# Four-layer graph network on one Trainium2 core: seven quarter products for the first linear product of layer 1

## What is computed

```python
h = jnp.maximum(_layernorm(x, axis=-1), 0.0)
def _gcn_layer(x, adj, W, b):
    support = jnp.einsum('bnf,fh->bnh', x, W)
    return jnp.einsum('bnm,bmh->bnh', adj, support) + b
h = jax.nn.relu(_gcn_layer(h, adj, W1, b1))
h = jax.nn.relu(_gcn_layer(h, adj, W2, b2))
x = x + _gcn_layer(h, adj, W3, b3)
```

## Time and profile before

| | |
|---|---|
| median of 3 runs | 2630.46 us (2630.12 to 2632.95) |
| profiled execution | 2627.68 us, its span 2625.9 us |
| granted TensorE clock | 0.999 |
| busy, share of the span | PE 99%, PEld 83%, DVE 70%, ACT 54%, POOL 56% |
| layer 0 | to about 909 us |
| layer 1 | about 909 to 1609 us |
| layer 2 | about 1609 to 2235 us |
| layer 3 | to the end |

### The profile page before, as it was taken

One profiled execution on the slowest core, in us unless ns is written; L12 is line 12 of the kernel. 1 busy time (PEld: TensorE's weight loads), 2 busy tenths in 40 slices (PEclk: granted clock), 3 DMA queues, 4 the chain that ended last, 5 costly groups with the idle time before them and its releaser, 6 DMA issues.

```text
span 2625.9 us, 44958 instructions
## 1 busy us (share of the span) xinstructions
PE 2591.7 (99%) x12938; PEld 2173.1 (83%) x12938; DVE 1843.3 (70%) x4093; ACT 1406.1 (54%) x2623; POOL 1472.8 (56%) x2283
## 2 busy tenths in 40 slices
PE   7999999999999999999999999999999999999999
PEld 6888888888888888888888888888888887788887
DVE  8877777777777766666666666666667676677776
ACT  5443444434444555454545455666566665666665
POOL 6544454444444654333333335777777767877776
PEclk9999999999999999999999999999999999999999
DMA  3111111111111321111111112222222223444443
GB/s 117 55 47 40 38 42 38 42 44 38 35 41 38 98 85 51 52 50 52 50 52 50 52 50 87 84 93 76 98 76 96 78 80 118 134 140 152 151 136 120
DMA packets 145389, 195.25 MB, mean 74 GB/s; under 512 B 55475, under 2 KB 55475, under 8 KB 145334
## 3 DMA queue, kind: packets, MB, share of 16 engines
q1 hardware_dynamic: 138560, 183.55, 21.4%
q10 hardware_dynamic: 6774, 11.03, 1.3%
HBM read 127.42 MB, written 67.11 MB: 74 GB/s over the span
## 4 chain that ended last, share of the span: by engine, by line
PE 93%; DVE 2%; POOL 2%; issue 1%; ACT 1%; DMA 0%; ACTq 0%; POOLq 0%; DVEq 0%
PE ps L584 27%; PE ps L586 27%; PE ps L585 26%; PE ps L601 6%; PE ps L626 4%; PE ps L604 2%; POOL w_lo L1476 1%; DVE row_lo L1122 0%; ACT row_hi L842 0%; POOL row_lo L1476 0%; PE ps L765 0%; PE ps L772 0%; DMA raw<-w_t 0%; POOL x_res L1589 0%; DVE stats L1216 0%
## 5 line engine op out<-in xcount | busy, mean ns | idle before, releaser
L584 PE MATMUL ps<-w_hi,col_hi 128*128 128x512 f32 x2432 | 970.0, 399 | 4.9 <-DVE w_lo L1122 3.8
L586 PE MATMUL ps<-w_hi,col_lo 128*128 128x512 f32 x2432 | 950.3, 391 | 0.0
L585 PE MATMUL ps<-w_lo,col_hi 128*128 128x512 f32 x2432 | 948.4, 390 | 0.0
L584 PEld LDWEIGHTS ps<-w_hi,col_hi 128*128 128x128 f32 x2432 | 457.6, 188 | 98.4 <-issue 7.9
L586 PEld LDWEIGHTS ps<-w_hi,col_lo 128*128 128x128 f32 x2432 | 457.0, 188 | 98.9
L585 PEld LDWEIGHTS ps<-w_lo,col_hi 128*128 128x128 f32 x2432 | 458.4, 188 | 87.5
L842 ACT ACTIVATE col_hi<-ps 128x512 fp32r<-128x512 f32 (+1 forms) x512 | 291.1, 578 | 225.3 <-PE ps L604 116.0
L1500 POOL TENSOR_TENSOR var_eps<-moments,eps_ln 128x1 f32<-128x1 f32 x256 | 51.2, 200 | 481.0 <-DVE moments L1139 480.8
L1476 POOL TENSOR_TENSOR row_lo<-normed,row_hi 128x512 fp32r<-128x512 f32 x160 | 207.4, 1297 | 197.2 <-ACT row_hi L842 195.3
L601 PE MATMUL ps<-adj_both,row_hi 128*128 128x256 f32 x1024 | 246.6, 329 | 0.2 <-DVE deg L1177 0.2
L1126 DVE TENSOR_TENSOR wide<-ps,col_hi 128x512 f32<-128x512 f32 x256 | 175.5, 686 | 78.7 <-ACT col_hi L842 76.1
(11 more groups left out here) (181 smaller groups left out, 4798.6 us busy)
## 6 DMA issues: line engine op xcount, KB each, us to landing
out<-x_res SPq DMA_DIRECT2D x256, 256.0 KB, 2.0
x_in<-out SPq DMA_DIRECT2D x192, 256.0 KB, 2.8
x_res<-out SPq DMA_DIRECT2D x128, 256.0 KB, 3.2
x_in<-x SPq DMA_DIRECT2D x64, 256.0 KB, 2.6
adj_in<-adj_t SPq DMA_DIRECT2D x96, 64.0 KB, 2.3
raw<-wk ACTq DMA_DIRECT2D x14, 256.0 KB, 3.6
raw<-w ACTq DMA_DIRECT2D x12, 256.0 KB, 2.7
raw<-w_t ACTq DMA_DIRECT2D x10, 256.0 KB, 4.2
```

Of the source, the lines that this page charges most:

```text
L584: nc.tensor.matmul(out_ap, lhs_hi, rhs_hi, start=start, stop=False, **checks)
L585: nc.tensor.matmul(out_ap, lhs_hi, rhs_lo, start=False, stop=False, **checks)
L586: return nc.tensor.matmul(out_ap, lhs_lo, rhs_hi, start=False, stop=stop, **checks)
```

## The change

**Seven quarter products.** For each pair of slots u = (a, b) of layer 1, the 24 matmuls of lin0 with 512 columns become seven products of a 256 x 256 quarter of W1 (two rows of 128, `narrow`) with 128 rows of one side: six matmuls of 256 columns each. The blocks are the left and right half of the features of slot a and slot b; the products are named and combined as in layers 2 and 3.
- adj0: ACT copies the first half to wide and not to col_hi, DVE's adj0hi adds the second half there in one step; the new adj0c copies it to col_hi (ACT) and subtracts for col_lo (POOL), for odd slots only 256 columns.
- sums0 (DVE, four steps of 256 columns per pair), sumsplit0 (ACT and POOL, two halves of 512 columns each).
- bias0 per pair: two copies of 256 columns; the second half holds the difference of the two bias halves, made once on POOL.
- q1, p6, s5 (ACT copies of 256 columns out of PSUM), c11, c22, c12 (DVE, 256 columns each), rows0 (the rectifier on ACT, in two halves for odd slots), rows0hi (DVE, likewise).

**Orders.** order_gcn, last_gcn and last_hyper are new lists; those of the other layers stay.

**Weights.** In layer 0's last group four raw blocks are loaded at once; seven quarters (B11, B21, B22 and four differences T, made on DVE) are split there and then the eight blocks of W2 and W3: 15 splits in place of 12. The bias is prepared there. STAGING is told by step and not by place for layer 1, steps 9, 10 and 11 move from group 1 to group 15, and EARLY_AT puts the blocks that take the place of the quarters last; they wait for p4 of the last pair.

The diff, cut to its core (the lists of last_hyper, last_gcn and the counting of semaphores are left out):

```diff
+        ("resid", 0), ("p1", 0), ("q1", 0), ("p2", 0), ("adj0", 3), ("p6", 0), ("s5", 0), ("p5", 0), ("p7", 0),
+        ("bias0", 1), ("rows0", 0), ("c11", 0), ("p3", 0), ("adj0hi", 3), ("sums0", 1), ("p1", 1), ("c12", 0),
+        ("p2", 1), ("sumsplit0", 1), ("c22", 0), ("q1", 1), ("p4", 0), ("rows0hi", 0), ("rows0hi", 1),
+        ("rows0", 1), ("adj1hi", 0), ("resid", 1), ("stats_n", 0), ("c11", 1), ("adj0c", 3), ("c22", 1),
+        ("c12", 1), ("adj1hi", 1), ("adj1", 0), ("p6", 1), ("s5", 1), ("bias1", 0), ("p5", 1), ("resid", 2),
+        ("adj1", 1), ("p7", 1), ("rows0hi", 2), ("norm_n", 0), ("rows0", 2), ("stats_n", 1), ("p3", 1),
+        ("resid", 3), ("bias1", 1), ("lin1hi", 0), ("rows0", 3), ("lin1", 0), ("adj1hi", 2), ("p4", 1),
+        ("adj1", 2), ("bias1", 2), ("rows0hi", 3), ("lin1", 1), ("asplit_n", 0), ("adj2", 0), ("stats_n", 2),
+        ("adj2hi", 0), ("lin1hi", 1), ("adj1", 3), ("lin1", 2), ("stats_n", 3), ("adj1hi", 3), ("lin2", 0),
+        ("split_n", 0), ("lin1hi", 2), ("adj2hi", 1), ("bias1", 3), ("norm_n", 1), ("lin1hi", 3), ("adj2", 1),
+        ("split_n", 1), ("asplit_n", 1), ("lin1", 3), ("asplit_n", 2), ("adj2hi", 2), ("norm_n", 2), ("adj2", 2),
+        ("split_n", 2), ("lin2", 1), ("norm_n", 3), ("adj2", 3), ("split_n", 3), ("adj0_n", 0), ("adj0_n", 1),
+        ("adj2hi", 3), ("adj0c_n", 0), ("adj0hi_n", 0), ("adj0hi_n", 1), ("asplit_n", 3), ("adj0c_n", 1),
+        ("sumsplit0_n", 0), ("sums0_n", 0), ("bias0_n", 0), ("lin2", 2), ("lin2", 3), ("adj0_n", 2),
+        ("adj0c_n", 2), ("adj0hi_n", 2),
     ]
...
+               ("tra", 2), ("trb", 1), ("linb", 0), ("trb", 2), ("tra", 3), ("lina", 2), ("linb", 1), ("linb", 2)]
+PRODUCTS = [("p1", 0), ("p2", 0), ("p6", 0), ("p5", 0), ("p7", 0), ("p3", 0), ("p1", 1), ("p2", 1), ("p4", 0), ("p6", 1),
+            ("p5", 1), ("p7", 1), ("p3", 1), ("p4", 1)]
+NARROW = ("B11", "B21", "B22", "T1", "T3", "T2", "T4")
+NARROW_AT = [(4, 0), (4, 1), (4, 2), (4, 3), (1, 1), (1, 2), (1, 3)]
...
 STAGING = {
-    (1, 0): {26: "load0", 38: 0, 50: 1, 57: 2, 59: 3, 66: 4},
-    (1, 1): {8: 5, 12: "load1", 25: 6, 28: 7, 29: 8, 36: 9, 41: 10, 61: 11},
-    (1, -1): {9: "load2", 24: 12, 26: 13, 32: 14, 36: 15, 63: "load3", 66: 16, 68: 17},
+    (1, 0): {("adj1", 3): "load0", ("adj2", 1): 0, ("lin2", 0): 1, ("adj0_n", 0): 2, ("lin2", 2): 3, ("adj0_n", 2): 4},
+    (1, 1): {("p7", 0): 5, ("p6", 1): "load1", ("adj1", 2): 6, ("lin1", 2): 7, ("adj2", 0): 8},
+    (1, -1): {("p3", 1): 9, ("lin1", 0): 10, ("lin1", 1): 11, ("adj1", 3): "load2", ("lin1", 2): 12, ("lin1", 3): 13,
+              ("adj2", 0): 14, ("adj2", 1): 15, ("lin2", 2): "load3", ("score_n", 2): 16, ("p6_n", 0): 17},
...
+            def narrow(slot, half, lhs_hi, lhs_lo, op, start=False):
+
+                place, k = NARROW_AT[NARROW.index(op)]
+                for j in range(2):
+                    of = slice(j * 2 * P, (j + 1) * 2 * P)
+                    last = product(ps[:, slot, half, 0:2 * P], lhs_hi[:, j * P:(j + 1) * P], lhs_lo[:, j * P:(j + 1) * P],
+                                   w_hi[:, place, k, of], w_lo[:, place, k, of], start=start and j == 0, stop=j == 1,
                                    skip_group_check=True)
                 return last
...
+            def sevenths(g, name, u):
+
+                a, b = 2 * u, 2 * u + 1
+                if name == "p1":
+                    pe.wait_ge(s1["adj0_lo"], n(g, a))
+                    pe.wait_ge(s1["bias0"], 2 * g + u + 1)
+                    if first(g):
+                        wait_split(pe, block_end[0] + len(NARROW))
+                    last = narrow(b, 1, col_hi[:, a, 0:2 * P], col_lo[:, a, 0:2 * P], "B11")
+                if name == "p2":
+                    pe.wait_ge(s1["adj0_lo"], n(g, a))
+                    last = narrow(a, 1, col_hi[:, a, 2 * P:F], col_lo[:, a, 2 * P:F], "B21", start=True)
+                if name == "p6":
+                    wait_pair(pe, "copied", "p1", 1, g, u)
+                    pe.wait_ge(sp2["sum_lo"], 2 * nq(1, g, u) - 1)
+                    last = narrow(b, 1, narrow_hi(u)[:, 1, :], narrow_lo(u)[:, 1, :], "T2")
+                if name == "p5":
+                    pe.wait_ge(sp2["sum_lo"], 2 * nq(1, g, u) - 1)
+                    last = narrow(a, 0, narrow_hi(u)[:, 0, :], narrow_lo(u)[:, 0, :], "T1")
+                if name == "p7":
+                    wait_pair(pe, "copied", "p6", 1, g, u)
+                    pe.wait_ge(sp2["sum_lo"], 2 * nq(1, g, u))
+                    last = narrow(b, 1, narrow_hi(u)[:, 2, :], narrow_lo(u)[:, 2, :], "T3")
+                if name == "p3":
+                    wait_pair(pe, "copied", "p5", 1, g, u)
+                    last = narrow(a, 0, narrow_hi(u)[:, 3, :], narrow_lo(u)[:, 3, :], "B22")
+                if name == "p4":
+                    wait_pair(pe, "corners", "c22", 1, g, u)
+                    pe.wait_ge(s1["adj0_lo"], n(g, b))
+                    last = narrow(b, 1, col_hi[:, b, 2 * P:F], col_lo[:, b, 2 * P:F], "T4")
+                last.then_inc(sp2["products"], 1)
...
                     copy(adj_hi[:, t, :], adj_in[:, t, :]).then_inc(s1["asplit_hi"], 1)
-                if name in ("adj0", "adj1", "adj2"):
+                if name == "adj0":
+                    act.wait_ge(s1["adj0"], i)
+                    if first(g):
+                        act.wait_ge(s0["trb"], n(FULL, t))
+                    else:
+                        act.wait_ge(s1["row0_lo"], i - SLOTS)
+                    copy(blocks(wide[:, t, 0:F]), halves(t)[0]).then_inc(s1["adj0_half"], 1)
+                if name == "adj0c":
+                    act.wait_ge(s1["adj0_full"], i)
+                    copy(col_hi[:, t, own1(t)], wide[:, t, own1(t)]).then_inc(s1["adj0_hi"], 1)
+                if name in ("adj1", "adj2"):
                     act.wait_ge(s1[name], i)
                     copy(blocks(col_hi[:, t, :]), halves(t)[0]).then_inc(s1[name + "_hi"], 1)
-                if name in ("bias0", "bias1"):
-                    c = int(name[4])
-                    act.wait_ge(s1[f"adj{c}_lo"], i)
+                if name == "sumsplit0":
+                    u = t
+                    wait_pair(act, "sums", "s2", 1, g, u)
+                    copy(narrow_hi(u)[:, 0:2, :], narrow_pair(u, 0)).then_inc(sp2["sum_hi"], 1)
+                    wait_pair(act, "sums", "s4", 1, g, u)
+                    copy(narrow_hi(u)[:, 2:4, :], narrow_pair(u, 1)).then_inc(sp2["sum_hi"], 1)
+                if name == "bias0":
+                    a, b = 2 * t, 2 * t + 1
+                    act.wait_ge(s1["adj0_full"], n(g, b))
                     if first(g):
-                        act.wait_ge(s["b1_loaded"], 32)
-                    copy(ps[:, t, 1, :], b0a_bc[:, c, :]).then_inc(s1[f"bias{c}"], 1)
-                if name in ("lin0", "lin1"):
-                    c = int(name[3])
+                        act.wait_ge(s["b1_ready"], 33)
+                    copy(ps[:, b, 1, 0:2 * P], b0a_bc[:, 0, 0:2 * P])
+                    copy(ps[:, a, 0, 0:2 * P], b0a_bc[:, 0, 2 * P:F]).then_inc(s1["bias0"], 1)
+                if name == "q1":
+                    wait_pair(act, "products", "p1", 1, g, t)
+                    wait_pair(act, "sums", "s4", 1, g, t)
+                    copy(wide[:, 2 * t, 0:2 * P], ps[:, 2 * t + 1, 1, 0:2 * P]).then_inc(sp2["copied"], 1)
+                if name == "p6":
+                    wait_pair(act, "products", "p6", 1, g, t)
+                    copy(wide[:, 2 * t, 2 * P:F], ps[:, 2 * t + 1, 1, 0:2 * P]).then_inc(sp2["copied"], 1)
+                if name == "s5":
+                    wait_pair(act, "products", "p5", 1, g, t)
+                    act.wait_ge(sp2["sum_lo"], 2 * nq(1, g, t))
+                    copy(narrow_full(t, 3), ps[:, 2 * t, 0, 0:2 * P]).then_inc(sp2["copied"], 1)
+                if name == "rows0":
+                    u = t // 2
+                    if t % 2 == 0:
+                        act.wait_ge(s1["c12"], 2 * g + u + 1)
+                        relu(row_hi[:, t, :], wide[:, t, 0:F]).then_inc(s1["row0_hi"], 1)
+                    else:
+                        wait_pair(act, "products", "p4", 1, g, u)
+                        wait_pair(act, "corners", "c22", 1, g, u)
+                        relu(row_hi[:, t, 2 * P:F], narrow_full(u, 3))
+                        relu(row_hi[:, t, 0:2 * P], ps[:, t, 1, 0:2 * P]).then_inc(s1["row0_hi"], 1)
+                if name == "bias1":
+                    act.wait_ge(s1["adj1_lo"], i)
+                    copy(ps[:, t, 1, :], b0a_bc[:, 1, :]).then_inc(s1["bias1"], 1)
+                if name == "lin1":
                     act.wait_ge(s1[name], i)
-                    relu(row_hi[:, t, :], ps[:, t, 1, :]).then_inc(s1[f"row{c}_hi"], 1)
+                    relu(row_hi[:, t, :], ps[:, t, 1, :]).then_inc(s1["row1_hi"], 1)
...
+            def corners0(g, name, u):
+
+                a, b = 2 * u, 2 * u + 1
```

(47 more changed lines are left out.)

184 lines of the change are left out of this document (127 added, 57 removed), and 31 rows, old and new, of the table LEAK.

## The result

| | before | after |
|---|---|---|
| median of the runs | 2630.29 us (4 runs, 2628.12 to 2632.95) | 2655.23 us (4 runs, 2652.25 to 2656.18) |
| profiled execution | 2627.7 us, span 2625.9 | 2652.25 us, span 2650.1 |

The ratio is 1.0092, with a 95% interval of 1.0075 to 1.011. The forecast was 2619 us, and its range ended at 2629: the result lies outside it, on the side that had a chance of 0.06.

A forecast was written before the change was run, and what follows sets the result against it. PE's instruction stream was taken as the bound: -19.2 us on PE, +8 us of waits, about 0 for transitions, so -11.2 us and 2619 us against the median; forecast 2612 to 2625, range with two rivals 2607 to 2629.

The forecast's parts named there:

- what bounds the kernel now: Layer 1's loop: PE busy throughout a 43.94 us pass, so a group costs what PE's instruction stream costs.
- What a matmul costs: PE in layer 1, start to start: 0.228 us per 512-column matmul, 0.232 per pair of 256 and 128 columns.
- the change on PE: Layer 1: 10.94 us removed, 84 matmuls at 0.116 us (9.74) added; 1.20 us less per group, 19.2 over 16.
- The other engines: Layer 1 load per group: ACT about 27.5 us, DVE about 30, POOL 25, all below 43; none becomes the bound.
- The waits: Layer 1 loop: p6 of pair 0 0.2 us late, p7 0.05, p6 of pair 1 0.25; 0.5 per group, 8 total.
- Weights and transitions: Layer 0's last group with three more splits and one more DMA: charged 0, bounded at 3 us.
- Moved steps in the last group and layers 2 and 3: Three staged blocks in layer 1's last group: 1 to 2 us once if cover were gone; layers 2 and 3 unchanged.
- The short products expose the chain: Rival, layer 1: later sumsplit0 makes PE wait; a loss from 1.2 us per group, 2638 us at 1.7; chance 0.05.
- Loads don't overlap: Rival, PE: each 256-column matmul costs 0.221 us with its weight load, +122 us, 2753 us; chance 0.01.
- nothing waits: Rival: no waits in layer 1 and 0.113 us per 256-column matmul, -23 us, 2607.5 us; chance 0.2.
- the 256 costs 0.124: Rival, PE: 256-column matmuls cost 0.124 us, -8.4 us plus half the waits, 2626 us; chance 0.19.
- The signs: Right: period near 43.2 us, 256s 0.116 apart. Wrong: 0.12 or more, p6 gaps over 0.5, idle near 870 us.

The follow-up runs named there:

- Run 3: Changed kernel with three of each quarter product's six matmuls left out (half the contraction): 2658.3 us, period 44.72 us in ten of twelve passes.
- run 8: Changed kernel with run 5, run 6 and run 7 together, output correct: 2633.5 us, ratio to before 1.0019, period 43.47 us.
- run 1: Changed kernel with DVE's sums0 and rows0hi reading one input from PSUM instead of SBUF (other values): 2632.9 us, period 43.70 us.
- run 4: Changed kernel without loading W2 and W3 in layer 0's last group, splits reading W1's blocks instead: 2649.5 us, stretch 198.11 us.
- run 5: Changed kernel with the batch of loads and its splits one place later, each later load one split later: 2649.7 us, stretch 198.92 us.
- run 9: Run 8 with two step pairs exchanged in layer 0's last group, layer 2's staged blocks 3 to 8 later, POOL's residual behind adj0c: 2648.6 us.
- run 10: As run 9, but POOL's residual of slot 0 ahead of adj0c of slot 2: 2638.0 us, period 43.45 us.
- run 11: Run 8 with staged blocks 3 to 7 in group 1's second half, their loads two linear products ahead, block 8 in the last group: 2633.8 us.
- run 6: Changed kernel with corner sums c11, c12 and c22 written to free PSUM banks and read there: 2647.6 us, period 44.20 us.
- run 7: Changed kernel, layer 1 order only: ACT's q1 and pair 1's sum splits earlier, POOL's residual ahead of adj0c: 2638.6 us, period 43.67 us.
- run 2: Changed kernel with POOL's layer 1 residual cut from 512 columns to 2: 2650.7 us, period 44.40 us.

## Why the prediction was wrong

The forecast was -11.2 us, the spans differ by +24.2. Of the 35.4 us between them some 18 lie in the twelve passes (+0.8 us each in place of -0.7) and 17.7 in the stretch (+15.6 in place of -2.1, its three groups at -0.7). In a pass, 0.5 us are PE's stream and 1.06 the waits.

- *"So a group costs what PE's instruction stream costs"* (**what bounds the kernel now**): true of before, false of after. Run 3 shows it: 5 us less of stream, no gain.
- **What a matmul costs, the change on PE.** 0.116 us was mis-sized by 0.003 to 0.004: 84 steps at 0.119 to 0.120 make 0.3 us per group. Another 0.2 goes to first matmuls behind a change of block, 0.05 to 0.09 each, which I had not charged. In run 8, where hardly anything waits, a group takes 43.47; without its last gap of 0.2 before adj0 that is 43.27, against my 42.74. The change does save PE time: 0.7 us per group, not 1.2.
- **The other engines.** *"Eight sums and six corners of 256 at 0.42"* is the step that failed. The row that I took (L1270 in the earlier trace rows) reads one input from PSUM. The corners do so as well, and measured 0.42. The eight sums of sums0 read both from SBUF, and so does rows0hi's row_lo of the corners; beside POOL they took up to 1.5 us. DVE's load was 33.4 and not 30 us for that reason: in run 1 it is 29.7. The trace of before has no such step in layer 1's loop or in layer 3, where I looked, but it has one of the same width in layer 2, 32 times, by source line:

```profile
L1310 DVE SCALAR_TENSOR_TENSOR wide<-wide x32: 425/791/1501, 1621.2 to 2208.7; 128x256 f32<-128x256 f32 x32
```

- *"Denser than layer 1 will be. So no engine becomes the bound by its load"*: right in its letter, and of no use. Load was never the question; run 8's DVE has 31.6 us of load and its PE no idle time.
- **The waits.** I found p6 of pair 0 (0.2 us; measured 0.33), p7 of pair 0 (0.05; it was p3 that had 0.08) and p6 of pair 1 (0.25; measured 0.30): the places of the chain are right, and its sizes to 0.13 us. I missed adj1 of slots 0 and 1 and adj0 of slot 2, 0.80 us together. They are the lock's: run 1, which changes DVE's steps alone, takes them away and leaves mine. 1.56 us per group against 0.5.
- **Weights and transitions.** Charged 0 and bounded at 3 us, measured 15.6. This is the second step that failed, a term put at nothing. Two causes are shown: the lock (7.6 us, up to 9.3 with run 1's lower clock) and the loads in ACT's queue (3.3 us by the gap that went in runs 4 and 5). *"One more DMA ... waits for nothing new"* looked at the first batch; the second one, four loads at once, waits for POOL's seventh split. Before, each load waited for a split too, but singly and for the one three blocks back. And I had costed the stretch by load: POOL's window of 56 us holds 39.2 us after, as little as before (38.2); the load was fine and the order was not. The remaining 3 to 5 us come by subtraction. I take them for the chain of groups 0 and 1, with the staged blocks in it; runs 9 to 11 move these gaps about and don't remove them, so this stays open.
- **Moved steps in the last group and layers 2 and 3**: bounded at 1 to 2 us and 0; the passage from layer 1 to 2 went from 168.88 to 168.62 and the periods stayed. Right.
- **The rivals.** *The short products expose the chain* is what happened, with its point of decision (1.2 us of waits per group) passed at 1.56. It had a chance of 0.05 because layer 3 spoke against it. Layer 3's products last twice as long, which I had written down, and its sums read PSUM, which I had not seen. *Loads don't overlap* is refuted by 0.119 us per step, *nothing waits* by the 1.56 us, and *the 256 costs 0.124* lies about as far above the trace's 0.119 to 0.120 as my 0.116 below.
- **The signs.** The 256s stand at the edge of my 0.12. The gap before p6 of pair 1 has POOL as releaser, but 0.30 and not 0.5 us. New idle time is at 878 us (1.0) and 897 us (3.3).

## What to carry to other kernels

Price an elementwise step by a row with the same memories for its inputs, not only the same width, and ask of each new step with two SBUF inputs what POOL does at that moment; a sum written to a free PSUM bank costs the same, and the step that reads it there stays at 0.41 to 0.43 us (run 6). When products get shorter, walk the chain around them first: once it binds, a shorter stream gives nothing (run 3), while three changed places, two on ACT and one on POOL, gave 1.1 us per group (run 7); POOL's alone is worth 0.75 (runs 9 and 10). A batch of loads issued from a compute engine's queue wants its wait to be over, and its reader further on in the queue (in run 11, with two linear products between them, the gap of run 10 is gone); else the engine stands for the wait, the 1.8 us of issue and the landing.

## What the hardware showed

- A DVE step with two SBUF inputs waits for a running POOL step that reads SBUF, and also the other way round: 256 columns took 0.41 to 1.52 us on DVE, and two POOL steps 2.99 in place of 2.54 us. With one input in PSUM the spread was 0.408 to 0.426 us in 96 cases.
- 256-column matmuls that each load new weights start 0.119 us apart, 512-column ones 0.23.
- After PE had been idle for 3.9 us (run 10), it ran at the lower of its two clock levels: 512-column matmuls stood 0.43 us apart from 1001.29 to 1004.27, and the window reads

```profile
1000.80:1005.00 4.20, 4.17 (x11) 3.32 (x12) 1.38 (x2) 1.83 (x4) 3.15 (x4) 0.59 0.00 0
```

  with a granted clock of 0.59, the lower level (1.2 GHz) for most of it. That is 1.6 us on top of the gap (eight steps at 0.43 in place of 0.23). After the 3.3 us gap at 897 us it happened in runs 1, 2, 3 and 6, and not in run 7 or in the changed kernel's own profile; in runs 4, 5 and 11 it came 1.5 to 2 us behind gaps of 1.7 to 1.8 us.
